# Perceiver block on one core: query projections from rounded parts and a rotation split over two engines

## The chip, the core and the metric

The kernel runs as one program on one core of a Trainium2 chip. The metric is the device time of one execution in microseconds (us). A time for a kernel is the median of its runs. Five engines work side by side, each with its own queue of instructions: PE (TensorE, matmuls), DVE (VectorE), ACT (ScalarE), POOL (GpSimd) and SP (SyncE, which here issues the loads). They wait for each other through semaphores that the program sets by hand. The programmer also chose every address in on-chip memory by hand.

## What is computed

The reference runs six blocks over a latent array x of 256 tokens by 512 features, with a context of 4096 rows by 128: an attention over the context, a windowed self-attention, a mixture of 32 experts, a second attention over the context, a state-space block, and a feed-forward block with rounded weights. The change lies in the second attention over the context:

```python
q_hk = (hidden_q @ Wq.T).reshape(Bv, Sv, H, K)            # first projection, 16 heads of 128
q_big = jnp.einsum('bshk,hkq->bshq', q_hk, w_kc_q)        # second, to 384
q_big = _apply_rope(q_big, sin_q, cos_q)                  # x * cos + rotate_half(x) * sin
q_r = jnp.einsum('bshq,hqr->bhsr', q_big, W_qr)           # third, to 64
k_r = jnp.einsum('bld,hdr->bhlr', kv_r, W_kr)
scores = jnp.einsum('bhsr,bhlr->bhsl', q_r, k_r)          # 256 x 4096 per head
attn = jax.nn.softmax(scores, axis=-1)
```

## The kernel before, in words

Tokens are two tiles (NT) of 128, features four tiles (KT) of 128, context rows eight chunks (NCH) of 512. The blocks run one after the other. The second attention over the context has two stages. The **query stage** makes the three projections for the 16 heads (XH), and beside them the keys and the scores of the first pair of heads. The **attention loop** then runs over the 8 pairs (XP): while the exponentials of pair p are transposed and weigh the context rows, the scores of pair p + 1 are made.

Two kinds of product are used. A matmul of float32 operands shows in the trace as two MATMUL records. The other kind takes float32r operands, which are rounded, and shows as one record. There, each operand is split into a high part (a copy on ACT, which rounds) and a low part (the value less its high part), and three products are added: high by high, high by low, low by high. Keys, scores and weighted sums are made so (`wkrH`/`wkrL`, `kvTH`/`kvTL`, `keyH`/`keyL`, `qsH`/`qsL`, `pH`/`pL`, `kvH`/`kvL`).

In the query stage, the order on PE is written out by hand. For head n it is: `p1(n + 1)` (first projection, line 1612: four float32 matmuls from `wqX` and `xnT` into bank 6), then `p2(n)` (second projection, line 1621: three float32 matmuls from `kcq` and `qh`), on odd heads `p3` (third projection of a pair, line 1633), two key chunks at heads 2 to 5 (`KEYS_AT`, line 1642), and one chunk of the first pair's scores at heads 6 to 13 (`SCORES_AT`, line 1657). `stay_awake` (line 1401) issues idle matmuls that keep PE busy, here at heads 14 and 15 and ahead of the last `p3`.

What the other engines do for head n:
- ACT copies the output of `p1` out of the bank (`qh`, line 825), rounds the two key chunks (line 814), on even heads copies the ranks of a pair out (`ranks_out`, `qr`, line 818), and for the first two pairs rounds them (`qsH`, line 809).
- DVE rotates (`rotated`, lines 1158 to 1164): one product with the cosines from PSUM, four with the sines into `qm2`, and a sum of the two in on-chip memory (line 1164). Then it makes the low part of two key chunks (line 1169) or takes a chunk of scores out of PSUM with its row maxima (`scores_out`, line 1175: four instructions).
- POOL makes low parts: `kvL` once (line 603, 128x4096), `wkrL` (line 607) and `qsL` (line 609) of two pairs.
- SP loads `wqX` for head n + 2 once `p1(n)` is done, and `kcq` and `wqr`.

`p1(n)` waits for the copy of `p1(n - 1)` and for some `qr`; `p2(n)` waits for `qh` of its head and for DVE's products of head n - 1 (`qm_ready`); the rotation of head n waits for the sum of head n - 1 (`qb_ready`); `p3` waits for two sums. Ahead of the stage, ACT rounds the turned context (`kvTH`, line 798, chunks 4 to 7 after the two tiles of `xnT`) and then all of `kvr` (`kvH`, line 799), on which `kvL` waits. After the stage, ACT loads the table for the exponential and takes the first exponentials (line 840), then the last `qr`, the first key chunk of pair 1, and the first transposed weights (`pH`, line 864).

The scores of a pair lie in one tile of 2 heads x 2 token tiles x 4096 columns (`sp_`).

Of the kernel before, what the change touches and what calls it, by code (L numbers as in the profile page):

```python
# [44 lines left out]
SCORES_AT = {6 + c: c for c in range(NCH)}  # L45
# [48 lines left out]
def perceiver(nc, a, out):  # L94
    ctx = ExitStack()
    with ctx:
# [91 lines left out]
        sp_ = A("scores", [P, 2, NT, L])  # L188
# [325 lines left out]
        def _(pool):  # L514
# [113 lines left out]
            for p in range(2):  # L628
                low_parts(p)
# [370 lines left out]
        def _(dve):  # L1000
# [149 lines left out]
            dve.wait_ge(qtab_in, 32)  # L1150

            def rotated(n):
# [10 lines left out]
                dve.wait_ge(qm_ready, n + 1)  # L1163
                dve.tensor_tensor(qb[:, n % 4], qb[:, n % 4], qm2[:], ALU.add).then_inc(qb_ready, 1)
# [6 lines left out]
            def scores_out(p, c, e):  # L1171
# [3 lines left out]
                dve.tensor_scalar(sp_[:, h, q, c * CH:(c + 1) * CH], PS[:, 4 * q + h, :], 1.0, None, ALU.mult, ALU.max,  # L1175
# [221 lines left out]
        def _(pe):  # L1397
# [248 lines left out]
            p1(0, 0, 0)  # L1646
# [336 lines left out]
```

## Time and profile before

| what | us |
|---|---|
| median of 3 runs | 1043.91 |
| lowest, highest | 1041.44, 1048.77 |
| the profiled execution, whole | 1038.18 |
| its span, first to last instruction | 1036.5 |
| PE busy, share of the span | 984.7, 95% |
| DVE busy | 733.9, 71% |
| ACT busy | 576.4, 56% |
| POOL busy | 290.9, 28% |

The profiled execution lies 5.7 us under the median of the runs. Of it 1.7 us are outside the span. Busy time is an average over stages with different limits, and matmuls overlap in it. Positions below are us from the start of the span. The query stage goes from about 338 to 436 us.

### The profile page before, as it was taken

The page shows a single profiled execution, that of the slowest core. Times are in us where ns is not written, and L with a number is a line of the kernel's source. Part 1 is how long each engine was busy: PE and PEld are TensorE (multiplying, and loading weights), DVE is VectorE, ACT ScalarE, POOL GpSimd, SP SyncE. Part 2 cuts the span into 40 slices and gives each one's busy share as a digit, 9 for nine tenths or more (in the row PEclk, how much of TensorE's full clock was granted, in tenths as well). Part 3 has the DMA queues.
Part 4 walks back from the last instruction along what each step waited for, and adds up shares of the span by engine and source line. Part 5 has one row for each costly group of instructions (what it writes and reads, how often), then busy time and mean ns, then how long its engine had stood idle before and what let it go on. Part 6 is the DMA issues. An engine that isn't in the chain of part 4 may idle for free.

```text
span 1036.5 us, 17973 instructions
## 1 busy us (share of the span) xinstructions
PE 984.7 (95%) x6609; PEld 785.7 (76%) x6609; DVE 733.9 (71%) x1449; ACT 576.4 (56%) x1257; POOL 290.9 (28%) x210
## 2 busy tenths in 40 slices
PE   7989999999999799999999999999999999989996
PEld 5545689999997567588777878878888787968753
DVE  3666456555553679888887987978878777658566
ACT  3445344444442321287767767777677677946634
POOL 6910054444442300000002222422405422113412
PEclk9999999999999999999999999999999999999999
DMA  8560066665531333122003464524413203065100
GB/s 272 132 246 1 3 226 242 231 212 212 212 122 57 104 93 89 48 77 60 21 24 78 82 111 65 106 41 90 87 37 84 81 5 98 1 232 239 66 1 21
DMA packets 65981, 109.16 MB, mean 105 GB/s; under 512 B 19409, under 2 KB 44145, under 8 KB 64754
## 3 DMA queue, kind: packets, MB, share of 16 engines
q1 hardware_dynamic: 65906, 108.17, 35.2%
q8 instruction: 46, 0.75, 0.3%
q14 instruction: 29, 0.24, 0.1%
HBM read 103.24 MB, written 4.91 MB: 104 GB/s over the span
## 4 chain that ended last, share of the span: by engine, by line
PE 77%; DVE 13%; ACT 6%; issue 2%; DMA 1%; POOL 1%; SPq 0%; DVEq 0%; POOLq 0%; ACTq 0%
PE PS L1680 16%; PE PS L1553 12%; PE PS L1669 10%; PE PS L1657 8%; PE PS L1572 6%; PE PS L1642 4%; PE PS L1772 3%; DVE scores L1175 2%; PE PS L1694 2%; ACT scores L840 1%; PE PS L1453 1%; PE PS L1815 1%; PE PS L1612 1%; PE PS L1621 1%; DVE pL L1228 1%
## 5 line engine op out<-in xcount | busy, mean ns | idle before, releaser
L1228 DVE TENSOR_TENSOR pL<-PS,pH 128x512 fp32r<-128x512 f32 x256 | 175.9, 687 | 63.3 <-ACT pH L864 62.9
L864 ACT ACTIVATE pH<-PS 128x512 fp32r<-128x512 f32 x256 | 151.9, 596 | 100.0 <-PE PS L1669 100.0
L840 ACT ACTIVATE scores<-scores,nmX 128x512 f32<-128x512 f32 x256 | 185.3, 724 | 18.5 <-DVE nmX L1179 18.5
L1175 DVE TENSOR_SCALAR_CACHE_REDUCE scores<-PS 128x512 f32<-128x512 f32 x256 | 172.7, 683 | 14.7 <-PE PS L1657 14.3
L1680 PE MATMUL PS<-pH,kvH 128*128 128x256 f32 x512 | 164.5, 321 | 6.6 <-ACT xnT L849 6.6
L1669 PE MATMUL PS<-ident,scores 128*128 128x128 f32 x1024 | 157.0, 276 | 1.1 <-DVE pL L1228 0.9
L1680 PE MATMUL PS<-pL,kvH 128*128 128x256 f32 x512 | 143.9, 281 | 0.0
L1680 PE MATMUL PS<-pH,kvL 128*128 128x256 f32 x512 | 143.6, 281 | 0.0
L1669 PEld LDWEIGHTS PS<-ident,scores 128*128 128x128 f32 x1024 | 117.4, 140 | 31.7 <-issue 16.4
L1680 PEld LDWEIGHTS PS<-pH,kvH 128*128 128x128 f32 x512 | 96.7, 189 | 10.8 <-issue 10.6
L1680 PEld LDWEIGHTS PS<-pL,kvH 128*128 128x128 f32 x512 | 97.2, 190 | 0.0
L1680 PEld LDWEIGHTS PS<-pH,kvL 128*128 128x128 f32 x512 | 96.5, 188 | 0.0
L622 POOL TENSOR_TENSOR xn<-xn,winvB 128x1024 f32<-128x1024 f32 (+1 forms) x17 | 39.5, 2323 | 149.0 <-DMA xn<-in_w1t 91.2
L1082 DVE TENSOR_TENSOR gL<-rawG,gH 128x1536 fp32r<-128x1536 f32 x16 | 56.9, 3556 | 29.5 <-ACT gH L723 29.4
L607 POOL TENSOR_TENSOR wkrL<-wkr,wkrH 128x128 fp32r<-128x128 f32 x8 | 4.2, 524 | 247.2 <-ACT wkrH L804 247.1
L586 POOL TENSOR_TENSOR dL<-rawD,dH 128x1536 fp32r<-128x1536 f32 x16 | 56.4, 3526 | 47.2 <-ACT dH L767 47.2
L1657 PE MATMUL PS<-keyH,qsH 64*128 64x512 f32 x256 | 58.5, 454 | 6.2 <-DVE scores L1175 5.7
L1553 PE MATMUL PS<-xH,gH 128*128 128x256 f32 x192 | 54.5, 284 | 2.8 <-DVE uL L1082 2.4
L1657 PEld LDWEIGHTS PS<-keyH,qsH 64*128 64x128 f32 x256 | 24.0, 183 | 40.8 <-issue 24.5
L1553 PE MATMUL PS<-xH,uH 128*128 128x256 f32 x192 | 54.3, 283 | 0.0
L1553 PE MATMUL PS<-xL,uH 128*128 128x256 f32 x192 | 54.3, 283 | 0.0
L1553 PE MATMUL PS<-xH,uL 128*128 128x256 f32 x192 | 54.3, 283 | 0.0
(310 smaller groups left out, 2247.4 us busy)
## 6 DMA issues: line engine op xcount, KB each, us to landing
rawG<-in_wg SPq DMA_DIRECT2D x16, 768.0 KB, 5.6
rawU<-in_wu SPq DMA_DIRECT2D x16, 768.0 KB, 7.0
rawD<-in_wd SPq DMA_DIRECT2D x16, 768.0 KB, 6.2
wrow<-in_w SPq DMA_DIRECT2D x11, 512.0 KB, 4.1
xn<-in_w1t SPq DMA_DIRECT2D x11, 512.0 KB
wturned<-turned SPq DMA_DIRECT2D x4, 1056.0 KB, 13.3
wb<-w_rows SPq DMA_DIRECT2D x32, 128.0 KB, 3.3
wqX<-in_wqX SPq DMA_DIRECT2D x16, 256.0 KB, 2.6
```

The costliest lines, as they stand in the source:

```text
L586: pool.tensor_tensor(dL[:, b].rearrange("p m n -> p (m n)"), rawD[:, b], dH[:, b].rearrange("p m n -> p (m n)").bitcast(F32), ALU.subtract ...
L840: act.activation(at, at, ACT.Exp, bias=nmX[:, p % 2, h, q:q + 1], accum_out=csum[:, p % 2, NT * h + q, c:c + 1]).then_inc(exp_done, 1)
L864: act.activation(pH[:, i % 4], PS[:, 2 + i % 2, :].rearrange("p (k t) -> p k t", t=T), ACT.Copy).then_inc(pH_ready, 1)
L1082: dve.tensor_tensor(lo[b][:].rearrange("p k m n -> p (k m n)"), raw[:, b], hi[b][:].rearrange("p k m n -> p (k m n)").bitcast(F32), ALU.su ...
L1175: dve.tensor_scalar(sp_[:, h, q, c * CH:(c + 1) * CH], PS[:, 4 * q + h, :], 1.0, None, ALU.mult, ALU.max, accum_out=cmax[:, h, q, c:c + 1] ...
L1228: dve.tensor_tensor(pL[:, i % 4], PS[:, 2 + i % 2, :].rearrange("p (k t) -> p k t", t=T), pH[:, i % 4].bitcast(F32), ALU.subtract).then_in ...
L1553: mm = pe.matmul(PS[:, 3 * b + m, j * T:(j + 1) * T], w[b][:, kt, m, :], v[:, kt, :], start=(kt == 0 and c == 0), stop=(kt == KT - 1 and c ...
L1572: mm = pe.matmul(PS[:, 6 + t, :], h[:, b, m, t * P:(t + 1) * P], w[:, b, m, :], start=(first and m == 0 and c == 0), stop=(last and m == 2 ...
L1642: mm = pe.matmul(PS[:, bank, :], w[:, p % 2, :], v[:, c * CH:(c + 1) * CH], start=(j == 0), stop=(j == 2))
L1657: mm = pe.matmul(PS[:, 4 * q + h, :], w[rank, p % 2, q * P:(q + 1) * P], v[rank, c * CH:(c + 1) * CH], start=(j == 0), stop=(j == 2), skip ...
L1669: mm = pe.transpose(PS[:, 2 + i % 2, m * T + q * P:m * T + (q + 1) * P], sp_[:, h, q, tile * P:(tile + 1) * P], ident[:])
L1680: mm = pe.matmul(PS[:, 6, h * T:(h + 1) * T], w[:, 4 * c + 2 * u + m, :], v[:, i % 4, m, :], start=(i == 0 and m == 0 and k == 0), stop=(c ...
```

## The change

The diff has four parts, all in the query stage. First, `p1` takes its operands in high and low parts. ACT rounds the normalized input (`xtH`, two instructions of 128x512) and each head's weights (`wqH`, 16 of 128x512, made two heads ahead at the end of a head's work); DVE makes `xtL` (two of 128x512), and POOL `wqL` (16 of 128x512). `p1` becomes 12 float32r matmuls, and waits for `wqL` of its head. Second, the sum of the rotation goes from DVE to POOL, same tile and size (128x768), 16 of them. Third, the scores lie by chunk: seven chunks in one tile, and the last in a tile of its own, whose place is held by `xtH` and `wqH` until the last `p1` is done. The first scores start one head later (heads 7 to 14). Fourth, the idle matmuls of head 14 are gone, and those ahead of the last `p3` wait for a score tile.

```diff
-SCORES_AT = {6 + c: c for c in range(NCH)}
+SCORES_AT = {7 + c: c for c in range(NCH)}
...
         xn = sb("xn", [P, NT, D])
+        xtL = sb("xtL", [P, KT, T], F32R, early)
+        early.close()
         xnT = sb("xnT", [P, KT, T])
...
-        sp_ = A("scores", [P, 2, NT, L])
+        score_chunks = A("scores", [P, NCH - 1, 2, NT, CH])
+        early = ExitStack()
+        xtH = sb("xtH", [P, KT, T], F32R, early); wqH = sb("wqH", [P, 2, KT, XK], F32R, early)
+        early.close()
+        last_chunk = A("last_chunk", [P, 2, NT, CH])
...
+            def low_query(n):
+                pool.wait_ge(wH_ready, 2 * PAIRS + n + 1)
+                pool.tensor_tensor(wqL[:, n % 2], wqX[:, n % 2], wqH[:, n % 2].bitcast(F32), ALU.subtract).then_inc(d_ready, 1)
+
+            low_query(0)
+            low_query(1)
             pool.wait_ge(kvH_ready, 1)
             pool.tensor_tensor(kvL[:], kvr[:], kvH[:].bitcast(F32), ALU.subtract).then_inc(kvL_ready, 1)
...
+            def rotated(n):
+                pool.wait_ge(qm_ready, n + 1)
+                pool.tensor_tensor(qb[:, n % 4], qb[:, n % 4], qm2[:], ALU.add).then_inc(qb_ready, 1)
...
             for p in range(2):
-                low_parts(p)
+                low_ranks(p)
+            for n in range(XH):
+                if n + 2 < XH:
+                    low_query(n + 2)
+                rotated(n)
+                if n in (5, 7):
+                    low_turned((n - 5) // 2)
...
+            def high_query_weights(n):
+                act.wait_ge(wqX_in[n % 2], (n // 2 + 1) * 16)
+                act.activation(wqH[:, n % 2], wqX[:, n % 2], ACT.Copy).then_inc(wH_ready, 1)
+
             for c in range(NCH):
                 if c == 4:
                     for t in range(NT):
                         turned_tile(3, t, 4)
+                        half = slice(t * P, (t + 1) * P)
+                        act.wait_ge(xnT_ready, 3 * NT + t + 1)
+                        act.activation(xtH[:, :, half], xnT[:, :, half], ACT.Copy).then_inc(xH_ready, 1)
+                    high_query_weights(0)
+                    high_query_weights(1)
...
+                if n + 2 < XH:
+                    high_query_weights(n + 2)
             ranks_out(XP - 2)
...
+                if c == 4:
+                    for t in range(NT):
+                        dve.wait_ge(xH_ready, NT + t + 1)
+                        half = slice(t * P, (t + 1) * P)
+                        dve.tensor_tensor(xtL[:, :, half], xnT[:, :, half], xtH[:, :, half].bitcast(F32), ALU.subtract).then_inc(xL_ready, 1)
...
-                dve.wait_ge(qm_ready, n + 1)
-                dve.tensor_tensor(qb[:, n % 4], qb[:, n % 4], qm2[:], ALU.add).then_inc(qb_ready, 1)
...
+                    if SCORES_AT[n] == NCH - 1:
+                        dve.wait_ge(p1_done, XH)
...
-            def p1(n, i, b):
-
-                pe.wait_ge(wqX_in[b], (i + 1) * 16)
+            def p1(n, b):
+
+                pe.wait_ge(d_ready, PAIRS + n + 1)
                 wait(pe, qh_ready, n)
                 wait(pe, qr_ready, (n - 3) // 2)
                 for kt in range(KT):
-                    mm = pe.matmul(PS[:, 6, 0:T], wqX[:, b, kt, :], xnT[:, kt, :], start=(kt == 0), stop=(kt == KT - 1))
+                    for c, (w, v) in enumerate(((wqH, xtH), (wqH, xtL), (wqL, xtH))):
+                        mm = pe.matmul(PS[:, 6, 0:T], w[:, b, kt], v[:, kt], start=(kt == 0 and c == 0), stop=(kt == KT - 1 and c == 2))
                 mm.then_inc(p1_done, 1)
...
             pe.wait_ge(kvTL_ready, NCH)
-            p1(0, 0, 0)
+            pe.wait_ge(xL_ready, 2 * NT)
+            p1(0, 0)
...
-                if n >= XH - 2:
+                if n == XH - 1:
                     stay_awake(10, 7)
...
             keys(1, 0)
+            pe.wait_ge(sX_out, 4 * (NCH - 1) + 1)
             stay_awake(6, 0)
             p3(XP - 1)
```

How the instructions stand on POOL, from `kvL` on. Before:

```order
L603 TENSOR_TENSOR kvL<-kvr,kvH 128x4096
L627 MEMSET rounding 128x2
L607 TENSOR_TENSOR wkrL<-wkr,wkrH 128x128
L609 TENSOR_TENSOR qsL<-qr,qsH 128x256
L607 TENSOR_TENSOR wkrL<-wkr,wkrH 128x128
```

The same place on POOL in the changed kernel:

```order
L620 TENSOR_TENSOR wqL<-wqX,wqH 128x512 x2
L625 TENSOR_TENSOR kvL<-kvr,kvH 128x4096
L659 MEMSET rounding 128x2
L629 TENSOR_TENSOR wkrL<-wkr,wkrH 128x128 x2
L620 TENSOR_TENSOR wqL<-wqX,wqH 128x512
L641 TENSOR_TENSOR qb<-qb,qm 128x768
L620 TENSOR_TENSOR wqL<-wqX,wqH 128x512
L641 TENSOR_TENSOR qb<-qb,qm 128x768
```

Two low parts of query weights now stand ahead of `kvL`. The third, for head 2, and the sum for head 0 stand behind `kvL` and both `wkrL`.

On ACT, ahead of `kvH` and for the first heads. Before:

```order
L798 ACTIVATE kvTH<-PS 128x512 x4
L686 ACTIVATE xnT<-PS 128x4x128 x2
L798 ACTIVATE kvTH<-PS 128x512 x4
L799 ACTIVATE kvH<-kvr 128x4096
L804 ACTIVATE wkrH<-wkr 128x128 x2
L825 ACTIVATE qh<-PS 128x256 x4
```

The same place on ACT in the changed kernel:

```order
L846 ACTIVATE kvTH<-PS 128x512 x4
L724 ACTIVATE xnT<-PS 128x4x128
L842 ACTIVATE xtH<-xnT 128x4x128
L724 ACTIVATE xnT<-PS 128x4x128
L842 ACTIVATE xtH<-xnT 128x4x128
L834 ACTIVATE wqH<-wqX 128x512 x2
L846 ACTIVATE kvTH<-PS 128x512 x4
L847 ACTIVATE kvH<-kvr 128x4096
L852 ACTIVATE wkrH<-wkr 128x128 x2
L873 ACTIVATE qh<-PS 128x256
L834 ACTIVATE wqH<-wqX 128x512
```

Four instructions of 128x512 now stand between the first half of `kvTH` and `kvH`, and one `wqH` stands behind each `qh`.

## Rows read from the trace of the kernel before

**Rows 1.** the page, chain that ended last, by engine

```profile
PE 77%; DVE 13%; ACT 6%; issue 2%; DMA 1%; POOL 1%; SPq 0%; DVEq 0%; POOLq 0%; ACTq 0%
```

**Rows 2.** chain in order of time, heads 6 and 7; start us, us

```profile
386.66 0.87 DVE qb L1158
...
389.09 0.97 DVE qb L1164
...
392.50 0.87 DVE qb L1158
```

**Rows 3.** the same chain, heads 13 and 14

```profile
415.90 0.98 PE PS L1657 x6
416.88 1.92 PE PS L1612 x8
418.80 1.29 PE PS L1621 x6
420.09 1.45 PE PS L1633 x12
421.54 1.58 PE PS L1657 x12
```

**Rows 4.** the same chain, six fp32r matmuls 128x256 of the attention loop

```profile
442.69 0.71 PE PS L1680 x6
```

**Rows 5.** groups by line and form; after the bar: busy us, mean ns

```profile
L594 POOL TENSOR_TENSOR hw<-hu,wb 128x768 f32<-128x768 f32 x16 | 29.4, 1839 | 73.1 <-DVE hu L1122 71.5 <-DMA wb<-w_rows 1.6
L657 POOL TENSOR_TENSOR ua<-upto,avH 128x512 fp32r<-128x512 f32 x8 | 9.6, 1196 | 24.3 <-DVEq L1297 15.3 <-DVEq L1277 7.5 <-PE PS L1799 1.4
L798 ACT ACTIVATE kvTH<-PS 128x512 fp32r<-128x512 f32 x8 | 4.5, 599 | 7.0 <-DVEq L1142 7.0
```

**Rows 6.** lines 1158 and 1164, each apart; ns min/median/max, first and last start

```profile
L1158 DVE TENSOR_TENSOR qb<-PS,cosQ x16: 949/956/959, 345.7 to 432.7; 128x768 f32<-128x768 f32 x16
...
L1164 DVE TENSOR_TENSOR qb<-qb,qm x16: 957/959/3034, 348.2 to 435.3; 128x768 f32<-128x768 f32 x16
```

**Rows 7.** timeline of ACT and SP before head 0

```profile
332.51 0.44 SPq L392 DMA_DIRECT2D wqX<-in_wqX  x1
...
335.64 2.39 ACT L798 ACTIVATE kvTH<-PS 128x512 fp32r<-128x512 f32 x4
...
337.93 3.61 ACT L799 ACTIVATE kvH<-kvr 128x4096 fp32r<-128x4096 f32 x1
```

**Rows 8.** one tile, wqX, all its 16 loads

```profile
DMA to landing us min/median/max: 2.4/2.6/5.2
```

**Rows 9.** timeline of POOL, start of the stage

```profile
341.61 8.84 POOL L603 TENSOR_TENSOR kvL<-kvr,kvH 128x4096 fp32r<-128x4096 f32 x1 [7.90 <-ACT kvH L799]
350.58 1.01 POOL L607 TENSOR_TENSOR wkrL<-wkr,wkrH 128x128 fp32r<-128x128 f32 x1
...
366.73 0.45 POOL L607 TENSOR_TENSOR wkrL<-wkr,wkrH 128x128 fp32r<-128x128 f32 x1
```

**Rows 10.** timeline of PE, heads 0 to 4

```profile
345.45 1.89 PE L1612 MATMUL PS<-xnT,wqX 128*128 128x256 f32 x8
...
354.02 2.31 PE L1621 MATMUL PS<-qh,kcq 128*128 128x256 f32 x6 [2.40 <-DVE qm L1162]
...
358.40 1.89 PE L1612 MATMUL PS<-xnT,wqX 128*128 128x256 f32 x8
```

**Rows 11.** stretches: us, PE, PEld, DVE, ACT, POOL, PEclk, DMA, GB/s

```profile
350.00:354.00 4.00, 1.61 (x8) 1.10 (x7) 3.83 (x7) 0.38 (x1) 1.51 (x3) 1.00 0.45 115
354.00:358.00 4.00, 3.98 (x11) 3.21 (x12) 2.49 (x5) 0.30 (x1) 0.00 (x0) 0.58 0.13 32
```

**Rows 12.** the same chain, the first exponentials

```profile
435.90 2.01 ACT scores L840 x5
```

**Rows 13.** timeline around the first attention pair

```profile
436.33 1.52 PE L1633 MATMUL PS<-qb,xn 128*64 128x256 f32 x12
...
438.77 0.58 ACT L864 ACTIVATE pH<-PS 128x512 fp32r<-128x512 f32 x1
```

More of the change, by code:

```diff
@@ L131, in perceiver @@
         keys_room = sb("keys_room", [P, 2 * L], F32, early)
+        wqL = sb("wqL", [P, 2, KT, XK], F32R, early)
+        early.close()
+        early = ExitStack()
+        sb("keys_room2", [P, 2 * L], F32, early)
         wqX = sb("wqX", [P, 2, KT, XK], F32, early)
@@ L187, in perceiver, with score @@
         rounding = A("rounding", [P, 2])
-        sp_ = A("scores", [P, 2, NT, L])
+        score_chunks = A("scores", [P, NCH - 1, 2, NT, CH])
+        early = ExitStack()
+        xtH = sb("xtH", [P, KT, T], F32R, early); wqH = sb("wqH", [P, 2, KT, XK], F32R, early)
+        early.close()
+        last_chunk = A("last_chunk", [P, 2, NT, CH])
+        def score(h, q, c):
+            return last_chunk[:, h, q] if c == NCH - 1 else score_chunks[:, c, h, q]
         cmax = A("cmax", [P, 2, NT, NCH]); nmX = A("nmX", [P, 2, 2, NT]); csum = A("csum", [P, 2, 2 * NT, NCH]); recX = A("recX", [P, 2, 2 * NT])
@@ L601, in _, with low_ranks, low_turned, low_parts @@
             rstd(3)
+            def low_query(n):
[3 more added lines that the diff above has]
+            low_query(1)
             pool.wait_ge(kvH_ready, 1)
             pool.tensor_tensor(kvL[:], kvr[:], kvH[:].bitcast(F32), ALU.subtract).then_inc(kvL_ready, 1)
-            def low_parts(p):
+            def low_ranks(p):
                 pool.wait_ge(wkrH_ready, p + 1)
                 pool.tensor_tensor(wkrL[:, p % 2], wkr[:, p % 2], wkrH[:, p % 2].bitcast(F32), ALU.subtract).then_inc(wkrL_ready, 1)
+            def low_turned(p):
                 pool.wait_ge(qsH_ready, p + 1)
                 pool.tensor_tensor(qsL[:, p % 2], qr[:, p], qsH[:, p % 2].bitcast(F32), ALU.subtract).then_inc(qsL_ready, 1)
+            def low_parts(p):
+                low_ranks(p)
+                low_turned(p)
+            def rotated(n):
+                pool.wait_ge(qm_ready, n + 1)
+                pool.tensor_tensor(qb[:, n % 4], qb[:, n % 4], qm2[:], ALU.add).then_inc(qb_ready, 1)
             def round_columns(k):
@@ L628, in _ @@
             for p in range(2):
-                low_parts(p)
+                low_ranks(p)
+            for n in range(XH):
[4 more added lines that the diff above has]
+                    low_turned((n - 5) // 2)
             pool.wait_ge(qr_ready, XP)
@@ L838, in exps @@
                     act.wait_ge(nm_ready, 4 * p + 2 * h + q + 1)
-                at = sp_[:, h, q, c * CH:(c + 1) * CH]
+                at = score(h, q, c)
                 act.activation(at, at, ACT.Exp, bias=nmX[:, p % 2, h, q:q + 1], accum_out=csum[:, p % 2, NT * h + q, c:c + 1]).then_inc(exp_done, 1)
@@ L1174, in scores_out @@
                 dve.wait_ge(sX_ps, 2 * (p * NCH + c) + q + 1)
-                dve.tensor_scalar(sp_[:, h, q, c * CH:(c + 1) * CH], PS[:, 4 * q + h, :], 1.0, None, ALU.mult, ALU.max,
+                dve.tensor_scalar(score(h, q, c), PS[:, 4 * q + h, :], 1.0, None, ALU.mult, ALU.max,
                                   accum_out=cmax[:, h, q, c:c + 1]).then_inc(sX_out, 1)
@@ L1667, in turn @@
                     for m in range(2):
-                        tile = 4 * c + 2 * u + m
-                        mm = pe.transpose(PS[:, 2 + i % 2, m * T + q * P:m * T + (q + 1) * P], sp_[:, h, q, tile * P:(tile + 1) * P], ident[:])
+                        tile = 2 * u + m
+                        mm = pe.transpose(PS[:, 2 + i % 2, m * T + q * P:m * T + (q + 1) * P], score(h, q, c)[:, tile * P:(tile + 1) * P], ident[:])
                 mm.then_inc(t_done, 1)
@@ L1697, in _ @@
                 if n + 1 < XH:
-                    p1(n + 1, (n + 1) // 2, (n + 1) % 2)
-                if n >= XH - 2:
+                    p1(n + 1, (n + 1) % 2)
+                if n == XH - 1:
                     stay_awake(10, 7)
```

## The prediction

> **What bounds the kernel now.** I read the chain of waits first. Over the whole span it is PE's for 77% and DVE's for 13% [rows 1], so an edit pays only where one of the two is waited for. The change touches the query stage alone, some 100 us of 1036, so I read the chain there in order of time. With scores in the queue, DVE sets the pace: from the first product of one head (386.66) to that of the next (392.50) are 5.84 us, and in them lie 2.43 us of products, 0.97 of the sum of line 1164, and 2.44 for four score instructions, with no gap [rows 2]. PE is close behind: 1.92 for `p1`, 1.29 for `p2`, 1.45 for `p3` on every second head, 1.58 for a chunk of scores [rows 3], which is 1.92 + 1.29 + 0.73 + 1.58 = 5.5 us a head. Ahead of the scores nobody is full. There POOL's `kvL` holds 8.84 us from 341.61 on, and the keys wait for it [rows 9], and PE stands still until 354.02 for DVE's products [rows 10].
>
> **Part 1, `p1` from parts.** Six float32r matmuls of the same shape take 0.71 us [rows 4], so 12 take 1.42; with the step to the next block (0.13, my choice) 1.55. Before, 1.83 to 1.92 by the chain [rows 3], so about 0.35 us are saved a head. If the part-wise form ran no faster than 1.92, the sum would be 5 us higher; at 1.42 it is 1 lower.
>
> **Part 2, what the parts cost ahead of head 0.** ACT makes four more instructions of 128x512 before the second half of `kvTH`, at 0.60 each [rows 5]: 2.4 us. The second `wqX` is issued at 332.51 [rows 7] and lands by at most 5.2 later [rows 8], at 337.7, where ACT would be ready at 337.2: 0.5 more. Some 0.2 fall into ACT's idle time. So `kvH` starts near 340.7, not 337.93 [rows 7], and `kvL` near 344.4. DVE's two `xtL` and the later `kvTH` put `p1` of head 0 off by 3.5 us. I cost that at nothing, since `p1(2)` is covered by POOL, next; without that cover it would be the 3.5.
>
> **Part 3, the new wait of `p1(2)`.** It waits for `wqL` of head 2, and this stands on POOL behind `kvL` and both `wkrL`. `kvL` ends at 344.4 + 8.84 = 353.2; two `wkrL` at 0.45 uncrowded [rows 9] make 354.2; one 128x512 at 1.20 [rows 5] makes 355.5. Before, `p1(2)` started at 345.45 [rows 10]: 10 us late. Behind it on PE stands `p2(1)`, for which DVE waits. Step by step: `p1(2)` 1.55, `p2(1)` 1.5, DVE's products 2.6 with the hand-over, so `p2(2)` at 361.1 against 354.02 (+7.1). Then POOL adds head 1 (1.84 for 128x768) and makes `wqL` of head 4 (1.20) [rows 5]: `p1(4)` at 364.2 against 358.40 [rows 10], +5.8.
>
> **Part 4, the clock.** Between 350 and 354 PE was busy 1.61 of 4 us, and in the next 4 us the granted clock was 0.58 [rows 11], near the lower level of 1.2 GHz; `p2` took 2.31 us [rows 10] and not 1.29 [rows 3]. Now PE stands idle from about 348 to 355.5. I expect the lower level again for some 3.6 us after it, where `p1(2)` and `p2(1)` lie: 2 blocks of 1.4 doubled, less what the POOL work hides, +1.8. Both ends: 0 and 3. `p1(4)` is then at 366.0.
>
> The Trainium skill (TensorE: Matmul & The Clock Gate, Part 1) says that an idle TensorE falls back to 1.2 GHz and is given 2.4 GHz again only after sustained work. The trace agrees with 0.58 [rows 11], and by the rule this term is sure, by the row likely.
>
> **Part 5, heads 4 to 8.** Chunk 7 of the scores starts at 421.54 [rows 3], so chunk 0 started 7 x 5.84 earlier, 380.7, and `p1(8)` behind it at 382.2: 23.8 after `p1(4)`. Now head 6 has no scores (-1.58) and one cheaper `p1` counts (-0.35; others end in waits for `qr`, bound -1.4): 366.0 + 21.9 = 387.9. Chunk 0 moves behind `p1(8)` 1.55, a wait of 1.1 for the products of head 6, `p2(7)` 1.4, `p3` 1.44: 393.4.
>
> **Part 6, eight chunks.** The sum leaves DVE: 5.84 - 0.88 = 4.96 us a head. PE needs 1.55 + 1.39 + 1.58 = 4.52 and 1.44 on every second head, 5.24 on average. PE is late next, and sets the pace: 7 x 4.52 + 3 x 1.44 = 36.0, so chunk 7 is at 429.4 against 421.54: +7.9, where it was +12.7 at chunk 0. POOL has 1.84 + 1.20 = 3.04 us of work a head, under 5.24, and its sum is hidden behind DVE's scores. The queue of loads has the same order; a load (median 2.6 [rows 8]), the copy and the low part take 4.4 us of two heads' 10.
>
> **Part 7, the tail.** Before, `p1(15)`, two rounds of idle matmuls and two `p2` lay between chunk 7 and the last but one `p3`. Now chunk 7 (1.58), one round (2.2) and `p2(15)` (1.4) do: `p3` at 434.6, then 1.6 for `qr` and 1.3 for the table: exponentials at 437.9 against 435.90 [rows 12]. DVE takes the last chunk out (3.3 us with its maxima) just ahead of the rotation of head 15, which so starts at 435.3; products to 438.0, POOL's sum 1.84, `p3(7)` at 439.9 against 436.33, and `pH` by the same step at 442.3 against 438.77 [rows 13]: **+3.5 us**. The attention loop behind it has the same instructions. Scores by chunk have the same sizes, so I cost them at nothing; the new wait for a score tile ends before PE comes to it.
>
> The sum against the profiled execution: 1038.2 + 3.5 = 1041.7. The median of the runs lies 5.7 above that execution, so the forecast is 1043.9 + 3.5 = **1047.4**, within 1% of before. (A measurement of this kernel can tell about 1%, 10.4 us, from no change.)
>
> **The bound for POOL.** In the one case where DVE's sum ran beside `kvL` it took 3.03 us, the others 0.96 [rows 6]: 2.07 more. So POOL and DVE can block each other, and two more kinds of work now stand on POOL. Ends: 0 and 2.07 for each of POOL's two instructions a head. I take 0, since DVE's cosine products, the first of them beside `kvL` at 345.7, have one operand in PSUM and took 0.95 to 0.96 us all 16 times [rows 6].
>
> The Trainium skill (SBUF — State Buffer, on the shared port pair) says that a DVE instruction with two operands in SBUF and a GpSimd one that reads SBUF exclude each other for their whole length. The trace agrees: the sum started at 348.2 [rows 6]; blocked until `kvL` ended at 350.45 [rows 9], with 0.85 left to do, it would take 3.1 us, and took 3.03. By the rule only `xtL` is left to be blocked here.
>
> **Rivals.** (A) The clock stays up after the idle 7 us: the 1.8 go, 1045.6. For it: PE was busy only 40% of the stretch from 350 on and still had the full clock there [rows 11]. Against: the stretch behind it. (B) DVE binds throughout, and PE's wait in Part 3 is hidden: the stage gains 16 x 0.88 + 2.07 = 16.2 us, less 2.8 of Part 2, 1030.5, faster. For it: rows 2. Against: POOL's queue, and PE's 5.24 a head. (C) **Slower**: POOL becomes the bound, in the loop over heads, because its sums and low parts are lengthened beside DVE. It decides once POOL's 3.04 us a head pass PE's 5.24. At 0.9 more for each instruction POOL has 4.8 a head, the start and tail grow too, and I get +9.6, 1053.5; at 2.07 more, 7.2 a head, 14 x 2.0 + 5 = +33, 1077. For it: rows 6. Against: the second operand in PSUM. (D) The part-wise `p1` runs at the rate of the float32 records, 12 x 0.22 = 2.6: +1.1 a head, 1060. Against: rows 4.
>
> **Chances.** Forecast (+1 to +8) 0.60, A 0.22, B 0.05, C 0.10, D 0.03. Faster by over 1%: B, 0.05. Slower by over 1%: D and most of C, 0.09. Within 1%: 0.86. The range takes A's bound with p1 at its cheap end and the runs' scatter (2.5 below the median), 1040, and C at 0.9 each, 1054.
>
> **What would show it.** `kvL` at 344.4; `p1` of head 2 at 355.5, released by POOL; a granted clock near half behind it; `p1` blocks of 1.42 us; 5.2 us a head with scores, PE without idle time and DVE with; the first `pH` at 442. Wrong would be: `p1(2)` before 350, POOL instructions of 128x768 far over 1.84, or `p1` blocks over 1.7.

## The result and the profile after

The changed kernel takes 1045.88 us in the median of 20 runs (1042.16 to 1049.43), the kernel before 1041.71 in 20 runs beside them (1037.82 to 1048.77): ratio 1.0036, 95% interval 1.0022 to 1.0050. The first three runs of before had given 1043.91. The forecast was 1047.4, +3.5 against before; measured are +4.2 by the two medians and +3.7 by the ratio. The profiled execution of the changed kernel took 1042.69 us, with a span of 1041.0. Its page, busy time by engine:

```profile
PE 983.4 (94%) x6663; PEld 790.1 (76%) x6663; DVE 721.2 (69%) x1435; ACT 586.5 (56%) x1275; POOL 339.4 (33%) x242
```

DVE lost 12.7 us of work and POOL got 48.5, the 16 sums and 16 low parts; the whole did not move with either. To place the rest, I use one ruler in every trace below, since the blocks ahead reach the stage some us earlier or later from run to run: the **stage** starts at the first group of `kvTH` copies on ACT. "Counted" positions are behind that start, which was 330.69 before:

```profile
330.69 2.06 ACT L798 ACTIVATE kvTH<-PS 128x512 fp32r<-128x512 f32 x4 [6.97 <-DVEq L1142]
```

The timeline of ACT in the changed kernel:

```profile
334.21 2.06 ACT L846 ACTIVATE kvTH<-PS 128x512 fp32r<-128x512 f32 x4 [7.01 <-DVEq L1192]
...
341.64 2.04 ACT L846 ACTIVATE kvTH<-PS 128x512 fp32r<-128x512 f32 x4
343.55 3.64 ACT L847 ACTIVATE kvH<-kvr 128x4096 fp32r<-128x4096 f32 x1
...
439.47 0.72 ACT L890 ACTIVATE scores<-scores,nmX 128x512 f32<-128x512 f32 x1
...
443.73 0.60 ACT L914 ACTIVATE pH<-PS 128x512 fp32r<-128x512 f32 x1
```

So the stage is 439.47 - 334.21 = 105.3 to the first exponential (before 435.90 - 330.69 = 105.2 [rows 12]) and 109.5 to the first `pH` (before 108.1 [rows 13]). It begins 3.5 us later than before, ahead of anything that the change touches. The timeline of POOL, to be read beside [rows 9]:

```profile
340.58 2.50 POOL L620 TENSOR_TENSOR wqL<-wqX,wqH 128x512 fp32r<-128x512 f32 x2 [3.35 <-ACT wqH L834]
347.26 8.89 POOL L625 TENSOR_TENSOR kvL<-kvr,kvH 128x4096 fp32r<-128x4096 f32 x1 [4.18 <-ACT kvH L847]
...
356.27 0.87 POOL L629 TENSOR_TENSOR wkrL<-wkr,wkrH 128x128 fp32r<-128x128 f32 x2
357.10 1.27 POOL L620 TENSOR_TENSOR wqL<-wqX,wqH 128x512 fp32r<-128x512 f32 x1
358.32 1.82 POOL L641 TENSOR_TENSOR qb<-qb,qm 128x768 f32<-128x768 f32 x1
```

and of PE, beside [rows 10]:

```profile
346.13 0.55 PE L1668 MATMUL PS<-xtH,wqH 128*128 128x256 f32 x1 [5.21 <-DVE kvTL L1198]
...
358.42 0.58 PE L1668 MATMUL PS<-xtH,wqH 128*128 128x256 f32 x1 [3.57 <-POOL wqL L620]
...
365.38 1.53 PE L1677 MATMUL PS<-qh,kcq 128*128 128x256 f32 x6 [1.26 <-DVE qm L1217]
```

PE reaches `p1(2)` (358.42) and is released by the low part of its weights, which stood on POOL behind 8.89 us of `kvL`. The stretches there, columns as in [rows 11]:

```profile
346.00:350.00 4.00, 3.31 (x14) 3.07 (x15) 0.03 (x1) 1.97 (x4) 2.74 (x1) 0.50 0.00 0
350.00:354.00 4.00, 4.00 (x17) 3.64 (x17) 0.00 (x0) 1.02 (x2) 4.00 (x1) 0.50 0.34 81
354.00:358.00 4.00, 0.85 (x3) 0.33 (x1) 2.46 (x5) 0.63 (x1) 3.92 (x5) 0.93 0.30 99
358.00:362.00 4.00, 3.58 (x16) 3.51 (x17) 0.00 (x0) 0.39 (x1) 3.38 (x3) 0.58 0.00 0
```

The granted clock (the third number from the end) is 0.50 behind the idle 5.21 us, that is 1.2 GHz, and falls again behind the idle 3.57. The first fall is hidden: PE would have waited for POOL in any case. The chain in order of time, from chunk 0 of the scores (395.33) to chunk 7 (431.13), beside [rows 2, 3]:

```profile
395.33 1.58 PE PS L1714 x12
396.92 1.61 PE PS L1668 x12
398.52 1.30 PE PS L1677 x6
399.82 1.60 PE PS L1714 x12
...
404.33 1.45 PE PS L1689 x12
...
431.13 0.89 PE PS L1714 x4
```

Where DVE set 5.84 us a head, PE now goes from piece to piece with no gap: 431.13 - 395.33 = 35.8 us for seven heads, 5.11 a head. DVE is the one that waits, 0.4 to 0.6 us on every second head, as here ahead of a rotation:

```profile
420.75 0.96 DVE L1213 TENSOR_TENSOR qb<-PS,cosQ 128x768 f32<-128x768 f32 x1 [0.41 <-PE PS L1677]
```

### The profile page after: what moved, and what is told of

It reads as the page before. It is cut to its first block, busy times and chain, and to the rows that moved or that the text cites. A ratio compares the mean times of both kernels' runs of the same rounds, so it can differ in the third digit from the quotient of the medians.

```text
span 1041.0 us, 18119 instructions
## 1 busy us (share of the span) xinstructions
PE 983.4 (94%) x6663; PEld 790.1 (76%) x6663; DVE 721.2 (69%) x1435; ACT 586.5 (56%) x1275; POOL 339.4 (33%) x242
## 4 chain that ended last, share of the span: by engine, by line
PE 49%; DVE 8%; ACT 3%; issue 1%; POOL 0%; DVEq 0%; ACTq 0%; POOLq 0%
PE PS L1737 16%; PE PS L1726 10%; PE PS L1714 9%; PE PS L1698 3%; PE PS L1751 2%; PE PS L1830 2%; DVE pL L1283 2%; DVE scores L1228 1%; ACT scores L890 1%; PE PS L1873 1%; PE PS L1677 1%; PE PS L1668 1%; PE PS L1689 1%; PE PS L1746 1%; DVE keyL L1222 1%
## 5 line engine op out<-in xcount | busy, mean ns | idle before, releaser
L890 ACT ACTIVATE scores<-scores,nmX 128x512 f32<-128x512 f32 x224 | 162.2, 725 | 18.5 <-DVE nmX L1232 18.4
L1228 DVE TENSOR_SCALAR_CACHE_REDUCE scores<-PS 128x512 f32<-128x512 f32 x224 | 151.3, 683 | 13.0 <-PE PS L1714 12.5
L1726 PE MATMUL PS<-ident,scores 128*128 128x128 f32 x896 | 138.3, 276 | 0.8 <-DVE pL L1283 0.6
L1726 PEld LDWEIGHTS PS<-ident,scores 128*128 128x128 f32 x896 | 103.0, 140 | 27.7 <-issue 14.3
L1737 PEld LDWEIGHTS PS<-pH,kvH 128*128 128x128 f32 x512 | 96.7, 189 | 10.8 <-issue 10.6
L1608 PE MATMUL PS<-xH,gL 128*128 128x256 f32 x192 | 55.5, 289 | 0.0
L1608 PE MATMUL PS<-xL,gH 128*128 128x256 f32 x192 | 55.5, 289 | 0.0
```

The source lines that it names most:

```text
L890: act.activation(at, at, ACT.Exp, bias=nmX[:, p % 2, h, q:q + 1], accum_out=csum[:, p % 2, NT * h + q, c:c + 1]).then_inc(exp_done, 1)
L1228: dve.tensor_scalar(score(h, q, c), PS[:, 4 * q + h, :], 1.0, None, ALU.mult, ALU.max, accum_out=cmax[:, h, q, c:c + 1]).then_inc(sX_out, 1)
L1608: mm = pe.matmul(PS[:, 3 * b + m, j * T:(j + 1) * T], w[b][:, kt, m, :], v[:, kt, :], start=(kt == 0 and c == 0), stop=(kt == KT - 1 and c ...
L1737: mm = pe.matmul(PS[:, 6, h * T:(h + 1) * T], w[:, 4 * c + 2 * u + m, :], v[:, i % 4, m, :], start=(i == 0 and m == 0 and k == 0), stop=(c ...
```

## The experiments

Each ratio is against runs of before on the same chip, whose medians were 1041.67 to 1042.37. "Chunk 0" is the start of the first chunk of scores. Stage lengths, counted, from each profiled execution:

| kernel | median, ratio [95%] | chunk 0 | first exponential | first `pH` |
|---|---|---|---|---|
| before, three profiles | 1041.71 | 49.9, 50.9, 48.3 | 105.2, 106.2, 103.6 | 108.1, 109.0, 106.5 |
| changed, two profiles | 1045.88, 1.0036 [1.0022, 1.0050] | 61.1, 62.0 | 105.3, 106.2 | 109.5, 110.5 |
| changed, sum on DVE | 1049.37, 1.0067 [1.0045, 1.0090] | 61.7 | 110.1 | 114.8 |
| before, sum on POOL | 1046.05, 1.0031 [1.0009, 1.0053] | 54.0 | 107.8 | 111.7 |
| changed, kvL on DVE | 1042.40, 0.9990 [0.9970, 1.0011] | 55.6 | 99.8 | 104.1 |
| before, kvL on DVE | 1043.00, 0.9995 [0.9971, 1.0019] | 47.0 | 102.3 | 105.2 |
| changed, idle matmuls | 1046.03, 1.0033 [1.0011, 1.0056] | 61.9 | 106.1 | 110.4 |
| changed, kvL behind wqL(2) on POOL | 1046.47, 1.0044 [1.0029, 1.0059] | 65.1 | 109.3 | 113.6 |
| changed, last sum on DVE | 1043.16, 1.0011 [0.9991, 1.0031] | 61.9 | 106.1 | 109.5 |
| kvL on DVE, order, idle matmuls | 1039.02, 0.9972 [0.9950, 0.9995] | 55.5 | 99.7 | 103.9 |
| the same, last sum on DVE | 1035.60, 0.9935 [0.9912, 0.9958] | 54.8 | 99.0 | 102.3 |

Four of these profiles had a low clock 4 to 8 us behind the stage's start, ahead of anything that their edits change: the second of before, the sum on POOL in before, the idle matmuls, and the three edits with `kvL` on DVE (last row but one). There PE turns the context rows; 16 matmuls of 128x128 took 3.42 us, and 2.45 in the other profiles. Between the two first profiles of before, chunk 0 came 1.0 later by it. Differences between a profile of one kind and one of the other hold this error.

### Scatter: both kernels once more

No edit.

> The changed kernel once more, as the measure of scatter. The stage is taken from the first kvTH copy to the first pH copy on ACT: 108.1 us before (438.77 - 330.69), 109.5 us changed (443.73 - 334.21). Theory T (the stage alone costs 1.4 us; the other 3 us between the two profiled executions are a dip of the clock at 120 to 150 us that comes and goes): stage 109.5 within 0.5 again, clock in 120 to 150 us often 1.00, ratio to before about 1.0015. Rival U (the loss is steady and lies outside the stage): the dip at 120 to 150 us is there again, ratio 1.0035 to 1.004.

> The kernel before once more, for its stage and its clock ahead of the stage. Its first profile reached the stage at 330.69 us; five profiles of other kernels, which do the same work up to there, reached it at 331.75 to 337.13. Theory T (noise ahead of the stage): it is reached at 331 to 337 us now, and the stage is again 105.2 us to the first exponential, 108.1 to the first pH, within 1. Rival U (the changed layout slows what lies ahead of the stage): reached at 330.7 again.

> The kernel before a third time, one look, for the scatter of its stage: 105.2 and 106.2 us to the first exponential and 108.1 and 109.0 to the first pH so far, against 105.3, 106.2 and 109.5, 110.5 for the changed kernel. Theory T (the stage is 1.4 us longer in the changed kernel, and the clock in it makes the scatter of 1): to the first pH 108.0 to 109.1. Rival (the scatter of the stage is larger than the difference): 109.5 or more.

The changed kernel again took 1045.75 us, ratio 1.0026 [1.0005, 1.0047]; it reached the stage at 331.75. Its stage was 110.5 to the first `pH`, 0.9 longer than the first time, where I had expected 0.5 at most. The dips of the clock at 120 to 150 us do come and go, as theory T had it: of the three profiles of before the first has none, the second and third have two, and of the changed kernel's the first has two and the second one. The kernel before reached the stage at 335.24 in a whole of 1045.42 us, and at 333.49 in 1038.81, so the late start is scatter and not the change's. The stage of before scatters by 2.5 us, more than I expected (its third was 106.5, and both theories had 108.0 or more), and the clock does it. The stretches of the third profile where the first had 0.58 [rows 11]:

```profile
353.50:357.50 4.00, 1.59 (x8) 1.12 (x7) 3.83 (x7) 0.38 (x1) 0.89 (x1) 1.00 0.35 115
357.50:361.50 4.00, 4.00 (x19) 3.42 (x19) 3.22 (x7) 1.20 (x2) 0.00 (x0) 1.00 0.17 49
```

The same program with the same wait (2.41 us for DVE's products) lost the clock there in the first two profiles and kept it in this one. Up to that `p2` the first and the third agree within 0.02 us (23.33 and 23.32), and chunk 0 then comes 1.6 earlier: that is the price of this fall. By the means to the first `pH`, the stage is 110.0 changed and 107.9 before: +2.1, not the 1.4 that the first pair showed. The ratios 1.0026 and 1.0036 are 2.7 and 3.7 us; 2.1 lies within the interval of the second measurement, just under that of the first. Outside the stage no loss shows. From the first `pH` to the end of the span are 597.7, 599.4 and 597.2 us before, and 597.3 both times in the changed kernel, so the new layout of the scores costs nothing there. Whether the rest is the clock of the stage in runs that have no profile isn't settled.

### What the sum's move brings by itself

Changed kernel, sum back on DVE:

```diff
                 dve.tensor_tensor(qm2[LEFT:P, 2], big[0:LEFT, 2], sinQ[LEFT:P, 2], ALU.mult).then_inc(qm_ready, 1)
+                dve.wait_ge(qm_ready, n + 1)
+                dve.tensor_tensor(qb[:, n % 4], qb[:, n % 4], qm2[:], ALU.add).then_inc(qb_ready, 1)
...
-                rotated(n)
```

> The changed kernel with the sum of the rotation back on DVE; p1 stays in parts, the scores stay one head later. Theory T (the sum's move only pays from the eighth head on, where DVE has 5.84 us a head and PE 5.12): start as in the changed kernel, p1(2) released by wqL behind kvL, chunk 0 of the scores at the same place, then 5.7 us a head, so the eight chunks end some 4 us later; stage 109.5 + 4.5 = 114, whole +4.5 against the changed kernel (ratio to before 1.008). Rival C (POOL's sums beside DVE cost as much as they free): stage no longer than 110, ratio 1.004. Rival V (the sum on POOL also delays the head of the stage): chunk 0 comes earlier by over 1 us than in the changed kernel.

It came as theory T has it: chunk 0 at the same place (61.7), then 5.8 us a head again from chunk 1 on (35.0 for six heads), stage +4.8 against the mean of the changed kernel, median +3.5. So everything but the sum's move, above all `p1` in parts, loses 7.0 us against before: the wait for POOL is paid, and DVE's 5.84 us a head hide the cheaper `p1`. There was one thing besides. The row of line 1218, the sum on DVE, for all 16:

```profile
L1218 DVE TENSOR_TENSOR qb<-qb,qm x16: 958/959/2015, 357.8 to 445.1; 128x768 f32<-128x768 f32 x16
```

The 2015 ns is the sum at 396.53, beside a `wqL` on POOL at 396.45; one took 1.55 us at 392.33, beside `wqL` and `qsL`, and the first 1.52 at 357.76, beside `wqL` at 357.20. Left on DVE, the sum collides with the new low parts, in 3 of 16 cases. The start of the scores one head later stands in both kernels, and no run tests it alone.

Before, with the sum alone on POOL (`rotated` as a loop behind both `wkrL`, the two lines gone from DVE):

```diff
-                dve.wait_ge(qm_ready, n + 1)
-                dve.tensor_tensor(qb[:, n % 4], qb[:, n % 4], qm2[:], ALU.add).then_inc(qb_ready, 1)
...
+            for n in range(XH):
+                pool.wait_ge(qm_ready, n + 1)
+                pool.tensor_tensor(qb[:, n % 4], qb[:, n % 4], qm2[:], ALU.add).then_inc(qb_ready, 1)
```

> The kernel before with the sum of the rotation alone moved to POOL (scores still from head 6, p1 still in float32). Theory T (PE is late next once DVE has 4.96 us a head): PE then needs 1.92 + 1.29 + 0.73 + 1.58 = 5.5 us a head, so 8 heads gain (5.84 - 5.5) x 7 = 2.4 us; the first sum waits behind kvL (until 350.6, then 1.84: +1.0 in the rotation of head 1) and each sum ahead of a third projection is 0.9 longer; tail +1. Stage 108.1 + 1.0 - 2.4 + 1.5 = 108.2, ratio 1.000. Rival B (DVE was all that bound): 16 x 0.88 less, stage 95 to 98, ratio 0.988. Rival C (POOL lengthened): sums over 2.5 us, stage over 112.

The whole missed: 1.0031 where I expected 1.000. The half on PE's pace held: from the rotation of head 7 to that of head 13 are 33.2 us (before 35.0), 5.53 a head where I had 5.5 (before 5.84). That is 2.2 over seven heads, where I had 2.4. Rivals B and C have fallen. The start was mis-sized. POOL and DVE there:

```profile
355.29 1.80 POOL L630 TENSOR_TENSOR qb<-qb,qm 128x768 f32<-128x768 f32 x1
```

```profile
357.20 0.96 DVE L1174 TENSOR_TENSOR qb<-PS,cosQ 128x768 f32<-128x768 f32 x1 [5.12 <-POOL qb L630]
```

The sum of head 0 stands behind `kvL` (8.86 us) and both `wkrL`; DVE waits 5.12 us for it, and PE 4.35 for the products, with a low clock behind (`p2` took 2.90). Chunk 0 is 4.1 us later than in the first profile of before where I had 1; 1.0 of it is the low clock ahead of the edit (against the second profile of before, which has it too, it is 3.1). In the changed kernel that loss isn't paid twice: `p1(2)` waits in the same place anyway. So the parts don't add: by the medians +7.0 and +3.7 alone, +4.2 and +3.4 together.

### kvL off POOL

`kvL` goes from POOL to DVE, behind the last `kvTL`, in the changed kernel and then in the kernel before:

```diff
-            pool.wait_ge(kvH_ready, 1)
-            pool.tensor_tensor(kvL[:], kvr[:], kvH[:].bitcast(F32), ALU.subtract).then_inc(kvL_ready, 1)
...
+            dve.wait_ge(kvH_ready, 1)
+            dve.tensor_tensor(kvL[:], kvr[:], kvH[:].bitcast(F32), ALU.subtract).then_inc(kvL_ready, 1)
             dve.wait_ge(qtab_in, 32)
```

> The changed kernel with kvL made by DVE (it stands idle there for about 9 us) instead of POOL, where wqL of head 2 waits behind it. DVE should need 4 to 5 us for 128x4096 by its rate at 128x512 (0.60 us). Theory T (what the change loses it loses behind kvL on POOL): p1(2) no longer waits for wqL but for qh, at about 351 (after's position counted from its kvTH copy: 354.9), stage 109.5 - 3 = 106.5, ratio to before 0.997 to 1.000; with kvL ended by 349, the first rotation is not delayed by over 1 us. Rival W (the keys and the qr waits set the pace anyway): p1(2) earlier by 3 us but chunk 0 at the same place, stage 109.5. Rival X (the low clock goes on longer, because PE starts earlier out of idle): gain under 1 us and a granted clock of 0.5 until p1(3).

> The kernel before with kvL alone moved to DVE, the control for the run in which the changed kernel got the same. There it took 4.42 us on DVE and the stage became 5.5 us shorter, the median 3.4. Theory T (before, kvL cost only the wait of the second rotation's sum, 2.1 us, since p1 did not wait for POOL): stage to the first exponential 105.2 - 1.3 = 103.9, ratio 0.998 to 1.000, so that the changed kernel with kvL on DVE (0.999) is at most level with it in the median and 4 us shorter in the stage. Rival (the same gain in both: kvL is simply cheaper on DVE): stage under 101, ratio 0.996.

In the changed kernel `p1(2)` comes at 19.7 counted instead of 24.2 and the stage is 5.9 us shorter to the first `pH`; the median falls by 3.5, to that of before. The loss of Part 3 is so shown to be `kvL` on POOL, and rivals W and X have fallen; the gain is twice the 3 us that I expected. In the kernel before, the same edit shortens the stage by 2.7 against the mean of before. But its profile kept the clock at 1.00 from 2 to 40 us, and the only one of before that did so is the third: against that one it is 1.3 (105.2 and 106.5), as expected. The ratio is 0.9995. So most of the loss behind `kvL` is the change's own. With `kvL` on DVE in both, the change shortens the stage by 2.5 to the first exponential and by 1.1 to the first `pH` (104.1 against 105.2), where I had expected 4; the medians, 1042.4 and 1043.0, can't tell these two apart. One row of each engine in the changed kernel with `kvL` on DVE, and the row of `wkrL` there:

```profile
350.30 4.42 DVE L1203 TENSOR_TENSOR kvL<-kvr,kvH 128x4096 fp32r<-128x4096 f32 x1 [1.19 <-ACT kvH L844]
```

```profile
L626 POOL TENSOR_TENSOR wkrL<-wkr,wkrH x2: 456/2442/4427, 350.6 to 355.0; 128x128 fp32r<-128x128 f32 x2
```

DVE needs half of POOL's time. But the first `wkrL`, begun at 350.61, took 4427 ns instead of 456: it ended just behind `kvL` (354.72). That did not hold `wqL(2)` up here: its high part `wqH(2)`, which waited 2.30 us for its load, ended at 355.46, together with the second `wkrL`, and `wqL(2)` started at 355.54. PE still waited 1.23 us for it.

Would it have been enough to let `kvL` stay on POOL and put it behind `wqL(2)`?

```diff
                 if n + 2 < XH:
                     low_query(n + 2)
+                if n == 0:
+                    pool.wait_ge(kvH_ready, 1)
+                    pool.tensor_tensor(kvL[:], kvr[:], kvH[:].bitcast(F32), ALU.subtract).then_inc(kvL_ready, 1)
                 rotated(n)
```

> The changed kernel with kvL still on POOL, but behind wqL of head 2 (and ahead of the sum of head 0). Theory T (kvL's 8.9 us on POOL delay whatever stands behind them, and the sum of head 0 is as urgent as wqL(2)): p1(2) starts at 17 to 19 us behind the first kvTH copy (it was 24.2 and 24.3), but the second rotation waits for POOL's first sum and starts at 27.7 to 28 (it was 28.5 and 29.5); stage to the first exponential 104.3 to 105.5, median 0 to 1 lower than the changed kernel's. Rival R (only the wait for wqL(2) binds, as Part 3 of the prediction has it): second rotation 4 earlier, stage 101 to 102.

No, and it was worse than I expected: stage 3.6 longer, ratio 1.0044. ACT, POOL and PE:

```profile
354.60 0.63 ACT L834 ACTIVATE wqH<-wqX 128x512 fp32r<-128x512 f32 x1 [2.35 <-DMA wqX<-in_wqX]
```

```profile
356.53 8.86 POOL L664 TENSOR_TENSOR kvL<-kvr,kvH 128x4096 fp32r<-128x4096 f32 x1
365.35 1.80 POOL L638 TENSOR_TENSOR qb<-qb,qm 128x768 f32<-128x768 f32 x1
```

```profile
368.43 0.58 PE L1668 MATMUL PS<-xtH,wqH 128*128 128x256 f32 x1 [6.29 <-POOL wqL L620]
```

`wqH(2)` waits for its load, which is issued only when `p1(0)` is done. I had left that out: `wqL(2)` ends at 20.8 counted and `p1(2)` comes at 21.5 (357.30), where I had 17 to 19, and POOL stands idle for 4.10 us ahead of it. `kvL` then holds the first sum and `wqL(3)`, and the wait moved to `p1(3)`, longer. Rival R has fallen.

### The clock

```diff
+            stay_awake(22, 7)
             pe.wait_ge(kvTL_ready, NCH)
             pe.wait_ge(xL_ready, 2 * NT)
             p1(0, 0)
...
             for n in range(XH):
+                if n == 1:
+                    stay_awake(24, 7)
```

> The changed kernel with idle matmuls in PE's two long waits: 22 ahead of p1 of head 0, 24 ahead of p1 of head 2. Theory T (the clock falls in these waits and costs 1 to 2 us behind them): granted clock 1.00 from 10 to 35 us behind the first kvTH copy (it was 0.50 to 0.58 in three of five stretches), p1(2) at the same place (24.2 behind that copy), p2(1) 1.1 earlier, stage 1.1 to 2.1 shorter, ratio to before 1.001 to 1.0025. Rival (the low clock is hidden by the wait for wqL and the loop between DVE and POOL): clock up and stage within 0.4 of 105.3 to 106.2.

Nothing gained: 1046.03, stage 106.1, of which some 0.5 is the low clock ahead of the first edit (`p1(2)` at 24.8 counted). `p1(0)` and `p1(1)` ran at the full clock, which the wait for `wqL(2)` hid. And the clock fell again where it counts, behind 1.96 us without work:

```profile
349.40 5.34 PE L1456 MATMUL PS<-busyB,identE 128*128 128x512 bf16 x23
356.70 0.38 PE L1668 MATMUL PS<-xtH,wqH 128*128 128x256 f32 x1 [1.96 <-POOL wqL L620]
...
359.06 2.21 PE L1677 MATMUL PS<-qh,kcq 128*128 128x256 f32 x6
```

```profile
358.00:360.00 2.00, 2.00 (x9) 1.82 (x9) 0.00 (x0) 0.38 (x1) 1.66 (x2) 0.50 0.00 0
```

So the rival holds for the first fall, and for the second the edit did not do what it was to do; this run does not test its price. The profiles of before put it at 1.6 us there.

Next, `kvL` on DVE, and with it the first 22 idle matmuls and `wqL(2)` ahead of `wkrL`:

```diff
+            low_query(2)
             for p in range(2):
                 low_ranks(p)
             for n in range(XH):
-                if n + 2 < XH:
+                if n and n + 2 < XH:
```

> The changed kernel with kvL on DVE, the low part of head 2's query weights ahead of wkrL on POOL, and 22 idle matmuls ahead of p1 of head 0. The run with kvL on DVE alone had the stage at 99.8 us to the first exponential and a median of 1042.4; there wkrL stood 4.85 us beside kvL, and wqL(2) behind it. Theory T (what is left at the start is the clock, about 1 us, and the order on POOL, 0.7; from the first rotation on each head waits for POOL's sum, 4.49 us a head): first rotation 0.9 earlier, stage 98.5 to 99.2, median 1041.3, ratio 0.998. Rival (only the order or only the clock binds): stage within 0.4 of 99.8.

The profiled stage is 99.7, as the rival had it. But this profile had the low clock ahead of the edits:

```profile
336.88:340.88 4.00, 4.00 (x21) 3.30 (x20) 1.99 (x4) 2.25 (x4) 1.27 (x1) 0.60 0.97 314
```

`p1(0)` came at 13.0 counted, and at 12.1 with `kvL` on DVE alone. The last run of this section has the same edits up to the tail and a clock of 1.00 there. Its first exponential is at 99.0, within theory T's range and 0.8 ahead of `kvL` on DVE alone. It shows what binds: `p1(0)` runs at the full clock, the load for head 2 is issued at 14.0 counted, not 15.0, `wqL(2)` starts at 17.6, not 18.4, and `p1(2)` comes at 19.0, not 19.7. So once `kvL` is gone, the low clock ahead of `p1(0)` isn't hidden any more, since it puts off the load. The order on POOL has its part too: in the run with `kvL` on DVE alone the second `wkrL` ended at 18.3, together with `wqH(2)`, and behind it `wqL(2)` could hardly have started at 17.6. The two weren't run apart. The median is 3.4 under that of `kvL` on DVE alone, with intervals that overlap, and a mean granted clock over the 12 runs of each of 0.991 against 0.987. The stage explains some 0.8 of it, and the rest stays open.

### The tail

```diff
+                if n == XH - 1:
+                    dve.wait_ge(qm_ready, XH)
+                    dve.tensor_tensor(qb[:, n % 4], qb[:, n % 4], qm2[:], ALU.add).then_inc(qb_ready, 1)
...
-                rotated(n)
+                if n < XH - 1:
+                    rotated(n)
```

> The changed kernel with the sum of head 15 alone back on DVE. In the changed kernel POOL's last sum (1.81 us) stands between the last rotation and p3(7), and from the first exponential to the first pH it takes 4.3 us (2.9 before). Theory T: the last p3 and the first pH come 0.8 to 1.0 earlier, first exponential to first pH 3.3 to 3.5; whole 0.9 lower, below what the runs can tell. Rival (qr, the key chunk and the exponentials on ACT bind, not the sum): still 4.2 to 4.3.

From the first exponential to the first `pH` are 3.37 us now (4.26), as expected. The changed kernel ahead, this one behind:

```profile
439.51 1.81 POOL L641 TENSOR_TENSOR qb<-qb,qm 128x768 f32<-128x768 f32 x1 [3.97 <-DVE qm L1217]
...
441.42 1.51 PE L1689 MATMUL PS<-qb,xn 128*64 128x256 f32 x12 [1.49 <-issue]
```

```profile
438.80 0.96 DVE L1221 TENSOR_TENSOR qb<-qb,qm 128x768 f32<-128x768 f32 x1
439.86 1.51 PE L1693 MATMUL PS<-qb,xn 128*64 128x256 f32 x12 [0.60 <-issue]
```

The median came down by 2.7, three times what the profile shows, but the intervals overlap, so the runs can't tell it from the 0.9.

All four edits together:

> The run with kvL on DVE, wqL(2) ahead of wkrL and idle matmuls ahead of p1(0) (1039.0, ratio 0.9972), with the last sum on DVE too. Theory T: stage to the first exponential 99.7 again, to the first pH 103.0 (it was 103.9); median 1038 to 1039, ratio 0.996 to 0.9975. Rival (that run's median was low by scatter, since its stage was no shorter than that of the run with kvL on DVE alone, 1042.4): ratio 0.998 to 0.9995.

1035.60 us (6 runs, 1034.62 to 1037.90), ratio 0.9935 [0.9912, 0.9958]: lower than both kernels, by 6 and 10 us, and lower than theory T had it (0.996 at best). Why is open. The stage is 102.3 to the first `pH`, 5.5 shorter than before's mean, 7.7 shorter than the changed kernel's. Here PE still waits 1.56 us for `wqL(2)`, which waits for the load of its weights.

## Why the prediction was right

Counted from the stage's start, where the prediction's positions lie 330.7 lower:

- **Part 1.** 1.61 us for `p1` where I had 1.55; `p2`, `p3` and scores as before (1.30, 1.45, 1.59). Rival D, 2.6, has fallen.
- **Parts 2 and 3.** `kvL` started at 13.1 (I had 13.7), `p1(2)` at 24.2 and 24.3 (24.8), released by POOL. `p1(0)` was 3.4 and 3.6 late (I had 3.5), and that was hidden, as I had it. The run with `kvL` on DVE takes this wait away and gets the time back. The claim in Part 6 that the queue of loads is harmless held for the changed kernel only because `kvL` hid it: with `kvL` gone or moved, the load of `wqX` for head 2 is what `wqL(2)` waits for.
- **Part 4.** The clock fell behind `p1(2)` as forecast: 10.0 and 10.8 us from `p1(2)` to `p1(4)`, forecast 10.5. That it also fell ahead of `p1(0)`, where 5.2 idle us stand, I had not foreseen; it was hidden. It stretched the work there, so that PE stood idle for 3.57 and 5.88 us ahead of `p1(2)`, not for the 7 that I had. Rival A has fallen. That before's own clock is kept in some executions wasn't foreseen either, and it makes the difference of the stages larger in the mean.
- **Part 5.** From `p1(4)` to chunk 0: 26.9 and 26.8 us, forecast 27.4. Its step "one cheaper `p1` counts (-0.35; others end in waits for `qr`, bound -1.4)" was mis-sized: from `p1(4)` (368.43) to `p1(8)` (389.33) are 20.9, not 21.9, so nearly the whole bound of 1.4 came. Chunk 0 came 11.1 and 12.1 later than in the first profile of before (+12.7).
- **Part 6.** 35.8 us for seven heads, forecast 36.0, with PE full and DVE waiting. Against before, chunk 0 to the first exponential fell from 55.3 to 44.2 us, 11.1 gained; the forecast was 12.7 - 2.0 = 10.7. (The 2.0 is 0.4 too large by its own terms: 434.6 + 1.6 + 1.3 = 437.5, not 437.9. The +3.5 does not go through it.) Only 5.0 of the 11.1 come from the pace of the seven heads, where the forecast had 12.7 - 7.9 = 4.8. The other 6.0 lie behind chunk 7: the scores start one head later, so less of the heads' work is left behind them. The same order stands in the 11.1 by which chunk 0 is late. In the first profile of each, the changed kernel is 3.6 late at `p1(8)` (55.1 against 51.5), 1.6 at `p1(15)` (93.9 against 92.4), and level at the first exponential.
- **Part 7.** First exponential to first `pH` 4.26 (forecast 4.4, before 2.9), and the last sum on DVE gives 0.9 of it back. The stage to the first `pH` is +1.4 and +2.4 against the same profile, where I had +3.5; the means of all give +2.1.
- **The bound for POOL.** POOL's sum took 1807 to 1852 ns and its low part 1266 to 1297 all 16 times, beside DVE's products and scores, which read PSUM. Rival C has fallen, and 0 was the right end. Rival B has fallen: DVE's pace bound only for the eight heads with scores.

The idle matmuls of head 14, gone with the change, explain little of the gain: before, DVE waited only 0.25 us for the `p2` behind them.

```profile
428.54 0.96 DVE L1158 TENSOR_TENSOR qb<-PS,cosQ 128x768 f32<-128x768 f32 x1 [0.25 <-PE PS L1621]
```

So the sign, the place and the size of the three large terms hold: 12.7 later at chunk 0 (11.1 and 12.1), 10.7 gained from there to the first exponential (11.1), 1.5 lost in the tail (1.4). That the total agrees to 0.2 us is partly luck: the stage in the traces is 1.4 under the forecast, and the ratios 0.6 and 1.6 above the stage. The absolute forecast, 1047.4, is 1.5 over the median, because the median of before went down by 2.2 with more runs.

## What to carry to other kernels

Where an engine gets new work, look for the longest instruction already in its queue (here 8.9 us of `kvL`): what is urgent behind it can be late by as much. Here an engine that stood idle there (DVE) was the place for it. Then look for the next wait: `p1(2)` came 4.5 us earlier, not 8.9, since the load of its weights bound next. Two edits that make an engine wait in the same place don't add up, and one that frees a bound engine pays only over the stretch in which that engine is the bound. Give the last instance of a moved step back to the faster engine where a chain ends on it.

## What the runs showed of the hardware

- DVE and POOL block each other in both directions when neither has an operand in PSUM: `wkrL` on POOL took 4427 ns instead of 456 beside DVE's `kvL`, DVE's sum 2015 ns instead of 958 beside POOL's `wqL`. The Trainium skill (SBUF — State Buffer, "SBUF: two separate sides", on the shared port pair) says that of two such instructions the second waits until the first has ended. Both agree: `wkrL` ended 0.32 us behind `kvL`, and DVE's sum 0.8 behind `wqL`.
- 128x4096 took 4.42 us on DVE and 8.86 on POOL, the sum of 128x768 0.96 and 1.81.
- The granted clock fell to 0.50 behind only 1.96 us of idle time on PE, with idle matmuls ahead of it, and stayed at 1.00 behind 2.41 us in one of three executions of the kernel before, and behind 1.56 us in the last two runs with `kvL` on DVE. In the transposes at the stage's start it fell in 4 of 14 profiles, though all 14 have the same 1.17 and 0.34 us of idle time ahead of them.
